# Four transformer blocks on one core: the last group's second projection and second norm are made one body earlier

## The reference

```python
ada = silu(c) @ ada_w + ada_b                       # shifts, scales and gates
x = x + gate_a * (attention(modulate(norm(x), shift_a, scale_a)) @ o_w + o_b)
h = modulate(norm(x), shift_f, scale_f)             # the second norm
x = x + gate_f * (gelu(h @ f1_w + f1_b) @ f2_w + f2_b)   # the MLP, 144 -> 576 -> 144
```

## Time and profile before

| what | value |
|---|---|
| median of three runs | 1354.49 us |
| the profiled execution | 1355.53 us |
| its span in the profile | 1353.8 us |
| TensorE, weight loads, DVE, ACT, POOL busy | 90%, 57%, 76%, 65%, 23% of the span |
| mean granted TensorE clock | 0.945 of full speed |

### The profile page before, as it was taken

One profiled execution on the slowest core, in us unless ns is written; L12 is line 12 of the kernel. 1 busy time (PEld: TensorE's weight loads), 2 busy tenths in 40 slices (PEclk: granted clock), 3 DMA queues, 4 the chain that ended last, 5 costly groups with the idle time before them and its releaser, 6 DMA issues.

```text
span 1353.8 us, 36566 instructions
## 1 busy us (share of the span) xinstructions
PE 1215.6 (90%) x13060; PEld 772.5 (57%) x13060; DVE 1034.8 (76%) x2750; ACT 881.2 (65%) x2122; POOL 313.2 (23%) x446
## 2 busy tenths in 40 slices
PE   5866889999879999999999999999999999998886
PEld 3332445556546666666666666666666666666554
DVE  7557778899858888888888888888878888886632
ACT  1323558677657777777777777777767766776653
POOL 3011112222222222222222222222222222221111
PEclk9756779999989999999999999999999999999998
DMA  5542334433364455444444444444477777777300
GB/s 134 174 115 69 97 98 126 125 104 100 96 166 131 130 134 135 133 133 126 128 125 127 122 128 126 129 128 127 121 133 152 151 149 154 143 130 122 60 27 27
DMA packets 209410, 163.63 MB, mean 121 GB/s; under 512 B 82872, under 2 KB 187264, under 8 KB 209232
## 3 DMA queue, kind: packets, MB, share of 16 engines
q1 hardware_dynamic: 208032, 160.71, 48.7%
q10 hardware_dynamic: 1200, 0.59, 0.2%
HBM read 98.05 MB, written 62.41 MB: 119 GB/s over the span
## 4 chain that ended last, share of the span: by engine, by line
PE 60%; DVE 18%; issue 8%; ACT 7%; DMA 3%; SPq 3%; DVEq 0%; POOLq 0%; POOL 0%; ACTq 0%
PE lin L1641 11%; PE lin L1657 9%; PE o_bank L1594 8%; DVE maxima L1200 5%; PE score_bank L1531 5%; PE score_bank L1487 4%; PE st_bank L1562 4%; ACT h2T L794 2%; PE lin L1645 2%; DVE stats L1062 2%; PE lin L1627 2%; ACT p_room L808 2%; PE lin L1474 2%; ACT hT_last L789 2%; PE lin L1628 1%
## 5 line engine op out<-in xcount | busy, mean ns | idle before, releaser
L1200 DVE TENSOR_REDUCE maxima<-score_bank 128x4 f32<-128x512 f32 x512 | 328.8, 684 | 75.0 <-PE score_bank L1531 71.7
L808 ACT ACTIVATE p_room<-st_bank 128x512 f32<-128x512 f32 x512 | 276.9, 596 | 107.7 <-PE st_bank L1562 72.2
L709 POOL TENSOR_TENSOR part_low<-qk_rest,part_mid 96x512 bf16<-96x512 f32 x96 | 114.9, 1197 | 379.0 <-DVE part_mid L1183 379.0
L1641 PE MATMUL lin<-h2T,w_h 128*128 128x512 f32 (+1 forms) x320 | 171.0, 633 | 3.8 <-ACT h2T L794 2.3
L1657 PE MATMUL lin<-w_f,gelu 128*128 128x144 f32 (+1 forms) x1280 | 171.5, 289 | 0.8 <-DVE gated L1258 0.8
L1594 PE MATMUL o_bank<-p_room,v_room 128*32 128x128 f32 x4096 | 167.0, 281 | 0.0
L1657 PEld LDWEIGHTS lin<-w_f,gelu 128*128 128x128 f32 (+1 forms) x1280 | 162.1, 191 | 2.8 <-DVE gated L1258 1.6
L1531 PE MATMUL score_bank<-stack_room 62*128 62x128 bf16 x2048 | 104.0, 222 | 52.6 <-DVE qk_rest L1178 19.2
L914 ACT ACTIVATE gelu<-lin 128x512 f32<-128x512 f32 (+1 forms) x160 | 90.9, 589 | 83.7 <-PE lin L1645 83.1
L1531 PEld LDWEIGHTS score_bank<-stack_room 62*128 62x128 bf16 x2048 | 60.1, 95 | 126.8 <-issue 48.8
L1562 PE MATMUL st_bank<-stack_room 64*128 64x128 bf16 x2048 | 113.6, 220 | 13.9 <-DVE mod_rem L1310 4.1
(11 more groups left out here) (180 smaller groups left out, 2209.7 us busy)
## 6 DMA issues: line engine op xcount, KB each, us to landing
stack_room<-stack_dram SPq DMA_DIRECT2D x192, 256.0 KB, 5.9
stack_dram<-part_high SPq DMA_DIRECT2D x64, 288.0 KB, 3.7
gates<-gates_dram SPq DMA_DIRECT2D x64, 288.0 KB, 3.3
norm_room<-stack_dram SPq DMA_DIRECT2D x64, 256.0 KB, 6.1
stack_dram<-part_mid SPq DMA_DIRECT2D x64, 192.0 KB, 2.6
stack_dram<-part_high SPq DMA_DIRECT2D x64, 144.0 KB, 3.7
stack_dram<-part_mid SPq DMA_DIRECT2D x64, 96.0 KB, 2.7
stack_dram<-part_low SPq DMA_DIRECT2D x64, 96.0 KB, 2.2
```

Source lines behind the costliest of these rows:

```text
L709: eng.tensor_tensor(part_low[:, T, :], qk_rest[:, T, :], part_mid[:, T, :], ALU.subtract)\
L808: eng.activation(probs[:, i % PBUFS, :], st_bank[i % 2][:, :], ACT.Exp, scale=float(HD) ** -0.5)\
L1200: eng.tensor_reduce(maxima[:, b, CH * c:CH * c + CH], bank_of(f"S{i}")[:, :].rearrange("p (h k) -> p h k", h=CH), AX_X, ALU.max)\
L1641: eng.matmul(o, w_h[l][:, cols], h2T[:, :], start=True, stop=False)
```

## The change

Body 32 (AFTER) makes the whole second norm of group 31. On TensorE `project(31, 1)` moves ahead of `up(30)`, and the flips of group 31's rows stand behind `up(30)` and ahead of `down(30, 0)`. On DVE statistics, normalising and the split of the last features stand right behind the projection's gating, and ahead of the gating of the MLP of group 30. On POOL `rstd_of` comes ahead of the two additions of group 30's MLP. On ACT the modulation comes behind the gelus of group 30 and ahead of the load of the exponential's table. Body 33 keeps group 31's `up`, gelus and `down`. Bodies up to 31 are unchanged. The order of bank uses is rewritten to match.

```diff
+FIRST, AFTER = -3, NG
...
-    order = [("T2_0", Q), ("OD2", P), ("Q1", L), ("T2_1", Q)]
+    order = [("OD2", P)] if g == AFTER + 1 else [("T2_0", Q), ("OD2", P), ("Q1", L), ("T2_1", Q)]
...
+    order += [("PJ1", P)] if g == AFTER else []
     order += [("F0", Q), ("F1", Q)] + scores[6] + [("F2", Q), ("F3", Q)] + scores[7] + [("F4", Q)]
-    order += ([("N", L)] if late else []) + [("PJ1", P)] + scores[0] + [("mT3", g)]
+    order += [("T2_0", P), ("T2_1", P)] if g == AFTER else ([("N", L)] if late else []) + [("PJ1", P)]
+    order += scores[0] + [("mT3", g)]
...
# POOL
                 add_attention(P, 1)
+                if g == AFTER:
+                    rstd_of(P, 1)
                 add_mlp(Q, 0)
-                rstd_of(P, 1)
+                if g < AFTER:
+                    rstd_of(P, 1)
                 add_mlp(Q, 1)
...
# ACT
-                modulated(Q, 1, 0)
+                if g <= AFTER:
+                    modulated(Q, 1, 0)
...
-                modulated(Q, 1, 1)
+                if g <= AFTER:
+                    modulated(Q, 1, 1)
...
                 gelus(Q, (3, 4))
+                if g == AFTER:
+                    modulated(P, 1, 0)
+                    modulated(P, 1, 1)
...
# DVE
-                last_parts(Q, 1)
+                if g <= AFTER:
+                    last_parts(Q, 1)
...
                 residual(P, 1, 0)
+                if g == AFTER:
+                    statistics(P, 1)
+                    normalise(P, 1)
+                    last_parts(P, 1)
...
-                if not late:
+                if not late and g < AFTER:
                     statistics(P, 1)
...
-                if not late:
+                if not late and g < AFTER:
                     normalise(P, 1)
...
# TensorE
-                flip_rows(Q, 1, 0)
+                if g <= AFTER:
+                    flip_rows(Q, 1, 0)
                 flip_o(P, 2)
                 queries_keys(L, 1)
-                flip_rows(Q, 1, 1)
+                if g <= AFTER:
+                    flip_rows(Q, 1, 1)
...
+                if g == AFTER:
+                    project(P, 1)
                 up(Q, (0, 1))
...
-                project(P, 1)
+                if g == AFTER:
+                    flip_rows(P, 1, 0)
+                    flip_rows(P, 1, 1)
+                else:
+                    project(P, 1)
                 scores(J, 0)
```

More of the change, by code:

```diff
@@ L130, in uses_of @@
     return [(name, of) for name, of in order if ok(of)]
-FIRST = -3
 BODIES = range(FIRST, NG + 3)
```

## The result

The changed kernel takes 1347.37 us, the median of 13 runs (1343.77 to 1351.87), against 1354.49 us before, also a median of 13 (1349.08 to 1356.79). The ratio is 0.9953, with a 95% interval of 0.9943 to 0.9963, so the change saves 5.0 to 7.7 us and the kernel is faster. The forecast was 1347.8 us within 1346.0 to 1350.4.

A forecast was written before the change was run, and what follows sets the result against it. The prediction took the end to be a chain, not a load. Savings of 4.6 and 2.6 us summed to 7.2, giving 1347.3 us against the median; it took 1347.8, with a range of 1346.0 to 1350.4.

The forecast's parts named there:

- What bounds the kernel: The last 53.8 us, with PE busy 73% at clock 0.85: the end is a chain and not a load.
- Projection first: project(31, 1) ahead of up(30): costs PE nothing in sum, its 1.3 us being gone from behind up(30).
- The norm under up(30): Group 31's norm, gating to last normed copy: 6.3 us, all hidden by up(30) with 1.1 us to spare.
- The wait in front of down(30, 0): Ahead of down(30, 0): a new wait for the first half's modulation, which frees its bank at T + 2.4.
- T: The end of up(30), forecast at about 1322.7 us in the trace's own times.
- First saving: up(31) starts at T + 8.1 = 1330.8 instead of 1335.42: 4.6 us saved.
- The clock: In up(31): at the full clock it takes 6.4 us instead of 9.06, if the clock holds.
- Second saving: In up(31): 2.6 us if the clock holds, with bounds of -0.8 and 2.6.
- The first rival: Around down(30) the clock falls once, costing 1.7 us (1349.5), or 2.6 us if up(31) stays slow (1350.4); chance 0.20.
- theory B of e1: In e1: fillers delay flips or up, or flips let the clock fall; within 1 us of before or slower.
- Hidden things: Group 31's gates, needed 9 us after landing is counted, and both table loads, done by T + 6.7, hold up nothing.
- the rivals: Alternative outcomes; the one around down(30) reckons 3.4 us at 0.50 to cost half, 1.7 us; chance 0.20.

The follow-up runs named there:

- e1: Kernel before, with bfloat16 products that nothing reads added in TensorE's waits ahead of group 31's flips and ahead of up(31); 1352.8 us, ratio 0.9982.
- e2: Changed kernel with only the norm early: group 31's flips, modulation and last_parts back in body 33, behind down(30); 1349.51 us, ratio 0.9957 to before.
- e3: Changed kernel with ACT loading the exponential's table ahead of group 31's modulation instead of behind it; 1351.46 us, ratio 0.9969 to before.
- e6: Kernel before, with 24 and 16 flips of the identity as filler in the waits ahead of group 31's flips and up(31); 1352.42 us, ratio 0.9982.
- e8: e2 with nine filler products in the wait for the modulation ahead of up(31); 1349.35 us, ratio 0.9952 to before.
- e5: Changed kernel with group 31's flips and three of its five up tiles in the two empty score banks; 1344.67 us, ratio 0.9925 to before.

## Why the prediction was right

- **What bounds the kernel.** A chain without other groups' work to fill it. e1 and e2 each take one part of it away and gain what the chain says.
- **Projection first costs nothing.** Forecast 9.3 us from its start to the end of up(30); measured 9.31 (1312.34 to 1321.65).
- **The norm under up(30).** Forecast 6.3 us with 1.1 to spare, measured 5.7 with 1.6. The 0.6 too much is mostly one term: I took 2.10 us for normed rows and copy from a stretch in which the rows took 1.61, and they took 1.15. Since up(30) covers the norm, it changed nothing in the sum.
- **The wait in front of down(30, 0).** Forecast T + 2.4, measured T + 2.23, released by h2T; e3 shows that it is on the path.
- **up(31) starts** at T + 8.05; forecast T + 8.1. First saving 4.64 us, counted from the first product behind the last flipped attention rows (up(30) at 1313.42 before, the projection at 1312.34 after: 22.00 and 17.36 us); forecast 4.6.
- **The clock.** Forecast 6.4 us for up(31), measured 6.6. Second saving 2.45 us; forecast 2.6. The missing 0.2 lies between the first two tiles and the gelu that releases the third (0.62 us of wait ahead of 1332.71, against 0.41 in rows 3). The first rival (a fall near down(30), with 0.20 as my estimate of its chance) did not show in any of four profiles, and e6 speaks against theory B of e1, that flips let the clock fall: the clock stays at 1.00 there through 5.8 us of them. So the clock term came out by more than luck, but four profiles don't exclude a rare fall.
- **Hidden things stayed hidden.** Gates for group 31 were issued at 1329.58 and needed at 1339.00; both table loads ended at 1328.25, ahead of the gelu at 1331.97.
- **Sum.** 7.2 us forecast, 7.17 by the two profiles (4.64 and 2.45, and 0.08 in a shorter wait ahead of the projection). That the medians differ by 7.12 is closer than the runs can tell: their ratio says 5.0 to 7.7 us.

What was not right in it: for the second saving I gave -0.8 as lower bound, which takes off the whole length of a further slow stretch of 3.4 us. Such a stretch costs about half its length (1.66 us of 3.4 in e3), as the rivals reckon; that gives 0.9, and e2 paid 1.50. I also said that a measurement tells 0.2% from no change. Single runs of either kernel are spread over 8 us, 0.6%, and only many of them bring the interval to 0.1% on either side. And I took 0.5 us off the saving because the profiled execution's extra 1.04 us might lie in the slow stretch of the tail. A slow stretch does vary in length (3.4 us in most profiles, 6.8 in e1 and e8 for the same wait), but here the 1.0 us lay ahead of body 32. The split of the first saving that I wrote down for e2 (2.8 us norm, 1.8 us hidden modulation) left out what the flips cost in front of down(30): net of that, e2 and e8 put 4.0 of the 4.6 us on the early norm, 0.6 on the early flips. The flips' real worth is that they cut one wait of 2.30 us into two of 0.83 and 0.64, after which the clock holds: 1.5 us more.

## What to carry to other kernels

At the end of a pipelined loop the last two groups have nobody to fill their waits, so steps that are well placed inside the loop deserve an order of their own there: start the last group's serial chain (projection, norm) under the last long piece of TensorE work. Count each TensorE wait there twice, once as itself and once as the clock behind it: behind up(30) in this kernel, waits of 2.2 us and more were followed by 3.4 to 10.2 us at half the clock, and waits of 0.83 and 0.64 us with 5.2 us of products between them were not. (Ahead of the projection, 1.9 and 0.7 us with only a pair of flips between them were followed by 3.4 to 6.8 us at half the clock; the one wait of 1.66 us that ends at 1267.54 was not the earlier trace rows.) And when a phase ends, look which PSUM banks have become idle with it; spreading the tail over them (e5) gained 3.2 us more by the trace for a change of a few names.

## What the runs showed that I had not expected

**Flips held the clock.** 40 float32 flips of 128x128 in place of bfloat16 products kept the granted clock at 1.00 in one profile (e6), and each still took 0.11 us.

**Part of the spread between executions arises in the first 50 us.** ACT's second and third table loads belong to the head norms of the first group; ahead of them lies the setup with its loads. Their times in the kernel before and in the changed kernel (timeline of ACT, from 40 to 60 us):

```profile
44.06 1.28 ACT L821 ACT_TABLE_LOAD   x1
52.03 1.28 ACT L826 ACT_TABLE_LOAD   x1
```
```profile
41.88 1.28 ACT L829 ACT_TABLE_LOAD   x1
49.84 1.28 ACT L834 ACT_TABLE_LOAD   x1
```

In e3 the third load is at 53.62 and in e1 at 48.80, in code that is the same up to there; the table load of body 32, 1260 us later, is at 1315.11 and 1312.19, so 2.9 of those 4.8 us are still there. These two are the extremes of the twelve profiles at both places. Single executions are spread over 8 us, more than the profiles cover, so how much of that arises here stays open. Which of the setup's loads or waits makes it was not tried. From 400 to 960 us, in contrast, the two profiles run alike: the clock is 1.00, and the kernel before and the changed one stay 0.9 to 1.2 us apart throughout. For an edit of the tail, an interval inside one trace shows what takes a dozen runs of the whole to see.

**A fall of the clock had more than one price.** The same wait ahead of the projection or of up(30) was followed by 3.4 us at half the clock in eight profiles and by 6.8 us in two (e1 and e8), and the end of up(30) came 1.2 to 1.3 us later for it.
